# A four-layer transformer on one core: four weight products moved from the third feed-forward's shared tiles into the third attention, and one PSUM bank for both tiles of a pair there

## The reference

```
x = x + tanh(g_xattn[l]) * attention_l(layernorm(x), ctx)
x = x + tanh(g_ffn[l])   * ffn_l(layernorm(x))
```

```
scores = hidden[b] @ memory[b].T / 16 ; scores = where(mask, scores, -1e30)
attn = softmax(scores) ; out = attn @ memory[b]      (zero where no row is valid)
```

```
u = x @ Wup + bup
g = silu(u @ Wgate + bgate) * u
o = g @ Wdown + bdown
```

## Time and profile before

| | us |
|---|---|
| median of 3 runs | 967.28 (965.3 to 967.49) |
| profiled execution, its own time | 966.25 |
| its span, first to last instruction | 964.4 |
| TensorE matmul busy | 793.1 (82%) |
| VectorE busy | 619.4 (64%) |
| ScalarE busy | 427.7 (44%) |
| GpSimd busy | 330.3 (34%) |
| mean granted TensorE clock | 0.874 |

### The profile page before, as it was taken

The page is one execution under the profiler, slowest core; times in us unless marked ns, Lnnn a source line. Parts: engine busy times, 40 slices in busy tenths (PEclk is TensorE's granted clock), DMA queues, the critical chain, the costliest instruction groups (busy, mean ns, idle before and its releaser), DMA issues.

```text
span 964.4 us, 16889 instructions
## 1 busy us (share of the span) xinstructions
PE 793.1 (82%) x4572; PEld 512.1 (53%) x4572; DVE 619.4 (64%) x1467; ACT 427.7 (44%) x932; POOL 330.3 (34%) x598
## 2 busy tenths in 40 slices
PE   0599998988882268888879997999996989999990
PEld 0445554444441144658568875656664845666650
DVE  8488997678866757657522237378885777444445
ACT  0456666567760012223127765666664313333320
POOL 3000002235636542023855765200002484233340
PEclk9799999989996569555799997899999599999995
DMA  9410006999108960005444536200003122223217
GB/s 327 127 23 21 21 12 192 305 305 314 39 12 336 320 183 1 0 0 197 130 134 138 153 104 195 72 20 20 19 7 119 52 89 83 61 79 91 87 37 261
DMA packets 90278, 113.00 MB, mean 117 GB/s; under 512 B 11685, under 2 KB 81864, under 8 KB 89050
## 3 DMA queue, kind: packets, MB, share of 16 engines
q1 hardware_dynamic: 83434, 95.20, 32.6%
q0 software_dynamic: 6768, 16.86, 4.9%
HBM read 51.10 MB, written 58.42 MB: 114 GB/s over the span
## 4 chain that ended last, share of the span: by engine, by line
PE 60%; DVE 15%; issue 8%; ACT 7%; POOL 6%; DMA 2%; DVEq 1%; SPq 1%; POOLq 0%; ACTq 0%
PE ps L2084 9%; PE ps L1670 7%; PE ps L1660 6%; PE ps L2104 4%; PE ps L1975 4%; PE ps L1681 3%; POOL x_rows L547 3%; PE ps L1993 2%; PE ps L1968 2%; PE ps L1706 2%; PE ps L2051 2%; PE ps L1880 2%; PE ps L1893 2%; PE ps L1657 2%; PE ps L1693 1%
## 5 line engine op out<-in xcount | busy, mean ns | idle before, releaser
L769 ACT ACTIVATE probs_t<-ps 128x1024 f32<-128x1024 f32 x64 | 65.5, 1024 | 71.1 <-PE ps L1670 71.1
L611 POOL COPY work<-ctx_rows 128x256 f32 (+1 forms) x32 | 12.7, 399 | 212.1 <-PE ps L1681 212.1
L1149 DVE TENSOR_REDUCE row_max<-ps 128x8 f32<-128x1024 f32 x64 | 77.9, 1217 | 4.6 <-issue 2.4
L1155 DVE TENSOR_TENSOR work<-ps,row_max 128x1024 f32<-128x1024 f32 x64 | 77.7, 1214 | 3.4
L1512 DVE TENSOR_TENSOR ctx_cols<-ps,ctx_rows 128x512 f32<-128x512 f32 x54 | 37.3, 691 | 59.9 <-PE ps L2084 59.7
L1015 ACT ACTIVATE ctx_cols<-ctx_cols 128x256 f32<-128x256 f32 x54 | 22.5, 417 | 117.1 <-DVE ctx_cols L1512 117.1
L1670 PE MATMUL ps<-ident,work 128*128 128x128 f32 x512 | 70.0, 280 | 2.3 <-ACT work L763 2.1
L2084 PE MATMUL ps<-early,xt 128*128 x152 | 71.5, 593 | 0.0
L1670 PEld LDWEIGHTS ps<-ident,work 128*128 128x128 f32 x512 | 56.7, 142 | 17.3 <-ACT work L763 13.1
L588 POOL DMA_INDIRECT y_rows<-ctx_cols,w2d x38 | 37.5, 988 | 80.7 <-DMA y_rows<-ctx_cols,w2d 47.1
L2104 PE MATMUL ps<-early,ctx_cols 128*128 (+1 forms) x216 | 55.8, 381 | 4.2 <-ACT ctx_cols L1020 4.2
(11 more groups left out here) (331 smaller groups left out, 1977.5 us busy)
## 6 DMA issues: line engine op xcount, KB each, us to landing
x_rows<-pad_row SPq DMA_DIRECT2D x1, 17415.0 KB, 66.8
work<-x_rows SPq DMA_DIRECT2D x77, 129.0 KB, 2.1
x_rows<-pad_row SPq DMA_DIRECT2D x1, 7740.0 KB, 35.3
x_rows<-pad_row SPq DMA_DIRECT2D x1, 7611.0 KB, 92.2
early<-in_w3st SPq DMA_DIRECT2D x8, 512.0 KB, 6.2
work<-y_rows SPq DMA_DIRECT2D x16, 256.0 KB, 2.9
early<-y_rows SPq DMA_DIRECT2D x8, 512.0 KB, 7.3
late<-in_w2u SPq DMA_DIRECT2D x1, 2304.0 KB, 9.7
```

Source lines behind the costliest of these rows:

```text
L769: act.activation(probs_t[:, :, :], ps[:, 4:6, :], ACT.Copy).then_inc(sem("att.evac"), 1)
L1149: dve.tensor_reduce(row_max[:, u, 8 * c:8 * c + 8], scores(c), AX.X, ALU.max).then_inc(sem("att.max"), 1)
L1155: dve.tensor_tensor(probs[:, u, c, :].rearrange("p (h k) -> p h k", k=P), scores(c), row_max[:, u, 8 * c:8 * c + 8].unsqueeze(2).to_broadc ...
```

## The change

The first four products move out of the third feed-forward's loop. Each is cut into two halves (`fuse(e, halves)`); a half is one product with the bias rows and two with the weights. The first half of product 0 stands behind the first pair's scores; after that each pair's `attend_l2` holds one half, between the transposes and PV, except the last. ScalarE copies a product after the exponentials of the pairs t = 2, 6, 10 and 14. VectorE adds the four products' bias rows once, ahead of the router's `norm_rows`. The products use banks 2 and 3; both transposes of a pair now go to bank 5 and both PVs to bank 4, so ScalarE copies both transposes in one instruction, and VectorE's first add waits for both PVs. TensorE's and ScalarE's loops over the pairs are written out. The router's tiles 8 and 12, which use banks 2 and 3, wait for the last copy and the bias add.

```diff
         def fuse_bank(e):
-            return 6 if e < EARLY else e - EARLY
+            return 2 if e < EARLY else e - EARLY
+
+        def fuse_rows(e):
+            return ps[0:E3 + 1, 3 if e < EARLY else 7, 0:D]
...
             def evac_l2(t):
-                for u in range(2):
-                    act.wait_ge(sem("l2.tr"), t + u + 1)
-                    wait(act, sem("l2.pv"), t + u - 1)
-                    act.activation(pt_l2[:, u], bank(2 + u, P), ACT.Copy).then_inc(sem("l2.evac"), 1)
+                act.wait_ge(sem("l2.tr"), t + 2)
+                wait(act, sem("l2.pv"), t)
+                act.activation(pt_l2, bank(5, 2 * P).rearrange("p (s n) -> p s n", s=2), ACT.Copy).then_inc(sem("l2.evac"), 2)
...
-            tile_pairs(act, attention2, peel=2)
+                if t % 4 == 2:
+                    act.wait_ge(sem("kv.stored"), 32)
+                    product_out(t // 4)
+            for t in range(0, NT, 2):
+                attention2(t, t == 0, t == NT - 2)
...
-                if 5 <= i < 5 + EARLY:
-                    product_out(i - 5)
...
-                    dve.wait_ge(sem("l2.pv"), t + u + 1)
-                    add_gated(4, t + u, bank(4 + u, D), rc_l2[:, u:u + 1])
+                    dve.wait_ge(sem("l2.pv"), t + 2)
+                    add_gated(4, t + u, bank(4, (u + 1) * D, u * D), rc_l2[:, u:u + 1])
...
+            def add_rows(e):
+                upto(dve, "wp.mm", e + 1)
+                dve.tensor_tensor(brow[:, D:2 * D], fuse_rows(e), brow[:, D:2 * D], ALU.add).then_inc(sem("b3.row"), 1)
+
             dve.wait_ge(sem("kv.stored"), 32)
+            dve.wait_ge(sem("load.brow"), 32)
+            add_rows(EARLY - 1)
             for g in range(3):
                 norm_rows(5, xs2, g)
...
-                if i == 10:
-                    dve.wait_ge(sem("load.brow"), 32)
-                    add_rows(EARLY)
...
+            def fuse(e, halves=(0, 1)):
+                if 0 in halves:
+                    pe.wait_ge(sem(f"load.st{e % 4}"), 16 * (e // 4 + 1))
+                    if e == EARLY:
...
+                    elif 0 < e < EARLY:
+                        upto(pe, "wp.out", e)
+                up_t, ga = wst[:, e % 4, 0], wst[:, e % 4, 1]
+                for c in halves:
+                    mm(fuse_rows(e), bupz[:, e, c, :], ga[:, c, :], start=(e in (0, EARLY) and c == 0),
+                       stop=(e in (EARLY - 1, E3) and c == 1), skip_group_check=True)
+                    for j in range(2):
+                        op = mm(ps[:, fuse_bank(e), c * D:(c + 1) * D], up_t[:, j, c * P:(c + 1) * P], ga[:, j, :], start=(j == 0),
+                                stop=(j == 1))
+                if 1 in halves:
+                    op.then_inc(sem("wp.mm"), 1)
...
+            def attend_l2(t, half):
+                if t == 0:
+                    pe.wait_ge(sem("resid3"), NT)
+                wait(pe, sem("l2.evac"), t)
                 for u in range(2):
                     pe.wait_ge(sem("l2.exped"), t + u + 1)
-                    wait(pe, sem("l2.evac"), t + u - 1)
-                    pe.transpose(bank(2 + u, P), p_l2[:, u], ident[:, :]).then_inc(sem("l2.tr"), 1)
+                    pe.transpose(bank(5, (u + 1) * P, u * P), p_l2[:, u], ident[:, :]).then_inc(sem("l2.tr"), 1)
+                if half:
+                    fuse(half // 2, (half % 2,))
+                pe.wait_ge(sem("l2.evac"), t + 2)
+                wait(pe, sem("resid4"), t)
+                for u in range(2):
+                    mm(bank(4, (u + 1) * D, u * D), pt_l2[:, u], ctx_rows[:, t + u, :], start=True, stop=True).then_inc(sem("l2.pv"), 1)
...
+            for t in range(0, NT, 2):
                 for u in range(2):
                     front(4, t + u, u, lambda u: pe.wait_ge(sem("front.out"), FRONT[3] + NT))
-                if not first:
-                    attend_l2(t - 2, isinstance(t, int) and t == 2)
+                if t:
+                    attend_l2(t - 2, t // 2)
...
-            tile_pairs(pe, attention2, peel=2)
-            attend_l2(NT - 2)
+                if t == 0:
+                    fuse(0, (0,))
+            attend_l2(NT - 2, 0)
...
+                    if L == 5 and t == 7:
+                        upto(pe, "wp.out", EARLY)
+                    elif L == 5 and t == 11:
+                        pe.wait_ge(sem("b3.row"), 1)
...
-                if 4 <= i < 4 + EARLY:
-                    fuse(i - 4)
```

More of the change, by code:

```diff
@@ L888, in evac_l2, with product_out @@
             def evac_l2(t):
-                for u in range(2):
-                    act.wait_ge(sem("l2.tr"), t + u + 1)
-                    wait(act, sem("l2.pv"), t + u - 1)
-                    act.activation(pt_l2[:, u], bank(2 + u, P), ACT.Copy).then_inc(sem("l2.evac"), 1)
+                act.wait_ge(sem("l2.tr"), t + 2)
+                wait(act, sem("l2.pv"), t)
+                act.activation(pt_l2, bank(5, 2 * P).rearrange("p (s n) -> p s n", s=2), ACT.Copy).then_inc(sem("l2.evac"), 2)
+            def product_out(e):
+                upto(act, "wp.mm", e + 1)
+                act.activation(w13[:, e, :, D:2 * D], bank(fuse_bank(e)).rearrange("p (j n) -> p j n", j=2), ACT.Copy
+                               ).then_inc(sem("wp.out"), 1)
             def attention2(t, first, last):
@@ L918, in score @@
                                ).then_inc(sem("rt2.sig"), 1)
[L920 to L923, removed]
             route_in(5, score)
@@ L1465, in _ @@
             hidden2(2)
-            def add_rows(n):
-                upto(dve, "wp.mm", n)
-                dve.tensor_tensor(brow[:, D:2 * D], ps[0:E3 + 1, 7, 0:D], brow[:, D:2 * D], ALU.add).then_inc(sem("b3.row"), 1)
             for i in range(NT + 2):
@@ L1498, in _ @@
             dve.wait_ge(sem("b3.row"), 1)
-            add_rows(E3 + 1)
+            add_rows(E3)
             for t in range(2, NT, 2):
@@ L1868, in _ @@
             pe.wait_ge(sem("mask.add"), 1)
-            def attend_l2(t, first=False):
+            def fuse(e, halves=(0, 1)):
+                if 0 in halves:
+                    pe.wait_ge(sem(f"load.st{e % 4}"), 16 * (e // 4 + 1))
+                    if e == EARLY:
+                        upto(pe, "s2.x", N2)
+                        upto(pe, "m2.h", NT + N2)
+                        upto(pe, "m2.ht", NT + N2)
+                    elif 0 < e < EARLY:
[9 more added lines that the diff above has]
+                    op.then_inc(sem("wp.mm"), 1)
@@ L1871, in attend_l2 @@
+            pe.wait_ge(sem("load.brow"), 32)
+            def attend_l2(t, half):
+                if t == 0:
+                    pe.wait_ge(sem("resid3"), NT)
+                wait(pe, sem("l2.evac"), t)
                 for u in range(2):
                     pe.wait_ge(sem("l2.exped"), t + u + 1)
-                    wait(pe, sem("l2.evac"), t + u - 1)
-                    pe.transpose(bank(2 + u, P), p_l2[:, u], ident[:, :]).then_inc(sem("l2.tr"), 1)
-                for u in range(2):
[L1876 to L1880, removed]
@@ L1889, in attention2 @@
                     wait(pe, sem("l2.exped"), t + u - 1)
-                    pe.wait_ge(sem("mask.add"), 1)
                     mm(bank(u, P), ones3[0:1, :], mask_bf[0:1, t + u, :], start=True, stop=False)
@@ L1940, in router @@
                 pe.wait_ge(sem("front.out"), FRONT[L] + NT)
[L1942 to L1951, removed]
-                up_t, ga = wst[:, e % 4, 0], wst[:, e % 4, 1]
-                for j in range(2):
-                    mm(ps[0:E3 + 1, 7, 0:D], bupz[:, e, j, :], ga[:, j, :], start=(e in (0, EARLY) and j == 0),
-                       stop=(e in (EARLY - 1, E3) and j == 1), skip_group_check=True)
-                for c in range(2):
-                    for j in range(2):
-                        op = mm(ps[:, fuse_bank(e), c * D:(c + 1) * D], up_t[:, j, c * P:(c + 1) * P], ga[:, j, :], start=(j == 0),
-                                stop=(j == 1))
-                op.then_inc(sem("wp.mm"), 1)
             def turn_slot(L, s, xd):
```

1 line of the change is left out of this document (removed).

## The result

On the chip of the first measurement the changed kernel takes 978.27 us (median of 4 runs, 977.01 to 980.96), the kernel before 966.29 (4 runs, 965.07 to 967.49): ratio 1.0128, 95% interval [1.0099, 1.0156]. It was measured twice more, beside other experiments: 973.95 us (5 runs, ratio 1.0064 [1.0037, 1.0092]) and 975.54 us (6 runs, 1.0104 [1.0072, 1.0137]). The 15 runs have a median of 976.5 and reach from 970.0 to 981.7. It is slower, as forecast (974.5). Part of the spread has a cause that the profiles show (experiment 8).

A forecast was written before the change was run, and what follows sets the result against it. It took TensorE at the low clock to nearly fill the third attention's rounds, and the sends to pace the shared tiles. 966.25 + 3.3 (high-clock sum with restart) + 5.0 (low-clock rounds) = 974.6, stated as 974.5 us; range 964.5 to 983.

The forecast's parts named there:

- removal from the shared tiles: Third feed-forward's shared tiles: taking out 11.5 us of TensorE work gains 0, since the sends set the pace.
- half behind the transposes, a round: Third attention, high clock: the half product between second transpose and PV delays PV by 0.9 us a round.
- shared bank, a round, high clock: Third attention: VectorE's first add waits for both PVs, moving its later work by 0.46 us a round.
- clean round at the high clock: Third attention: a round carrying a half product takes 6.96 us at the high clock, against 5.62 before.
- three stalls for ScalarE's copy: Third attention: in three of six rounds TensorE waits for ScalarE's product copy, 0.35 us each, 1.05 together.
- parts at the low clock: Third attention: the clock is lost now and then, two of six rounds' worth at the low clock, +5.0 us.
- first PV, from the stage's first transposes: Third attention's start: product 0's two halves stand ahead of the first PV and delay it by 1.65 us.
- last PV to the first send: tail, bias add, router: Attention's end and router: -0.4 us tail, +0.41 bias add, -1 router's first tiles if the clock is still high.
- restart at the low clock: TensorE's restart behind the shared tiles: a longer pause may lengthen its low start, 0 to +1.8 us, taken as +0.4.
- rival 1: Third attention: the clock stays high all through, giving 969.6 us; chance 0.18.
- Rival 2: Third attention: the clock stays low all through, giving 986 us; chance 0.14 for low throughout or nearly.
- Rival 3: Third attention: half product falls into TensorE's wait, add-wait hidden, high-clock rounds 5.6 to 6.5 us, 958 to 963.5; chance 0.13.

The follow-up runs named there:

- experiment 8: The changed kernel, unaltered, measured and profiled a third time: 975.54 us, ratio 1.0104 to the kernel before.
- experiment 1: The kernel before without its first four products, their copies and the first bias add, nothing put elsewhere: 965.71 us, ratio 0.9989.
- experiment 3: The changed kernel with each half product ahead of the pair's transposes and ScalarE's product copy ahead of the exponentials: 967.7 us, ratio 1.0005.
- experiment 4: The changed kernel with the two PVs in separate banks again and both tiles' scores sharing bank 0: 969.13 us, ratio 1.0019.
- experiment 6: The changed kernel with the edits of experiment 3, experiment 4 and experiment 5 together: 963.83 us (ratio 0.9975), again 961.38 us (0.9938).
- experiment 2: The kernel before with only the bank edit (both transposes in bank 5, both PVs in bank 4), no product moved: 972.21 us, ratio 1.0053.
- experiment 5: The changed kernel with products 4 to 7 in the old bias-rows-first order and the bias add behind three norm_rows: 974.14 us, ratio 1.0074.

## Why the prediction was right, point by point

| step | predicted, us | measured, us |
|---|---|---|
| removal from the shared tiles | 0 | experiment 1: -2.1 to +0.1 (interval) |
| half behind the transposes, a round | +0.9 | +0.80 (experiment 3) |
| shared bank, a round, high clock | +0.46 | +0.43 to +0.44 (experiments 4, 6), +0.63 (experiment 2, one round) |
| clean round at the high clock | 6.96 | 6.87 |
| three stalls for ScalarE's copy | +0.35 each | +0.32 each |
| last round | 6.04 | 6.06, 6.04, 5.79 |
| parts at the low clock | +5.0 | +5.4, +5.4, +1.5 |
| first PV, from the stage's first transposes | +1.65 | +1.67 in all three |
| first PV, from the span's start | (same) | +1.9, +2.1, 0.0 |
| last PV to the first send: tail, bias add, router | -1.0 | -0.2 |
| restart at the low clock | +0.4 (0 to +1.8) | +1.0 |
| late products' order | none | +1.2 |

The stage was right in mechanism and nearly in size. From its first transposes to L1430 (L1434 in the changed kernel) it is 8.5 us longer in two profiles and 4.4 in the third, within the 4 to 12 that were to show. Where three numbers stand in a cell, they are the three profiles of the changed kernel, in order. The measured +5.4 is the 53.59 us from first to last PV, less the last round (6.06) and three clean rounds and three with a stall (3 x 6.87 + 3 x 7.19 = 42.18). "Two rounds' worth" came out as parts of four rounds. It was a choice between cases rather than a working, so that it fits the first two profiles is in part luck: the third (+1.5) shows that rival 1, the clock high throughout, nearly happened in one execution. Rival 2, low throughout, did not in any, and no round was low from end to end, so the price of such a round (9.5 us) was not measured. Against the kernel before on the same chip the medians are 12.0, 7.0 and 9.9 us slower; the forecast was 7.2.

The Trainium skill (TensorE: Matmul & The Clock Gate, Part 4: PE-mode transpose) says that transposes don't count as busy for the clock. The case that the prediction drew from it, low throughout, is in none of the three profiles; that speaks against the sentence here, but no run tests it by itself.

The sum for the second profile: 8.9 us at the first send (458.16 against 449.23), 8.7 at the restart, 9.7 after the routed tiles' low start, 10.9 behind the late products, and 10.7 at the end of the span; its own time, 977.01, is 10.8 over the 966.25 of before. The forecast had 8.3. Three terms were mis-sized. The router gained next to nothing, 0.2 us from the last PV to the first send where 1.0 stood: the clock was low from 442 us on, as it had been before, although the stage ahead of it was mostly at the high clock. The restart cost 1.0 us and not 0.4, and its reason was wrong: the low time doesn't follow the pause (last section). And the products were costed only in the place where they went; the same edit to `fuse` rewrote the four that stayed, by an order that stands in the diff, at 1.2 us.

Rival 3, which I gave 0.13, failed for the reason given against it: the half can't use TensorE's wait ahead of the transposes, because it stands behind them. Experiments 3, 4 and 6 show it from the other side. Each of the two edits alone brings the median back to within 0.2% of before, and the two together, with the products' old order, make the kernel 0.25 to 0.6% faster.

## What to carry to other kernels

Look for the idle time in the profile and put moved work ahead of the wait that makes it, not behind: here the same half product cost 0.80 us a round behind the transposes and nothing ahead of them, save once at the stage's start. Work taken out of a stage that another engine or a transfer paces is worth next to nothing, in both places tried here (11.5 us for at most 0.2%, and 11.5 us for 0.9). When the clock can be lost, read it before pricing a local saving: experiment 4's 3.3 us came with 8.6 against two profiles of the changed kernel and 4.5 against the third, by how long the clock was low in each.

## What the runs showed of the hardware

**The clock isn't told by busy time alone.** In the kernel before, rounds with TensorE busy 6.49 of 6.90 us stayed low for 44 us; in experiment 1 the same code was back at 1.00 for its last round. In experiment 4, four rounds with 20.43 us busy of 26.37 were at 1.00 throughout. In the changed kernel one execution held 1.00 over 26.71 us with 18.49 busy, and two others fell to 0.69 as the mean of a round. What decides which level a stretch gets was not settled by these runs.

**The low start after a pause does not grow with the pause.** The first 6 us of the routed tiles (windows of TensorE: busy, clock, DMA share, GB/s), of experiment 6 and of experiment 5:

```profile
496.45:502.45 6.00, 6.00 (x26) 0.77 0.42 114
```

```profile
508.61:514.61 6.00, 6.00 (x18) 0.51 0.42 113
```

Both stand behind 18.3 us of idle time, and one is low for 2.75 us, the other for 6. Before, with a pause of 4.3 us, it was 3.75; over ten profiles 2.75 to 6.0. Half of each such time is lost: the last routed tile came 66.9 us behind the restart after 2.75 us low, 67.3 after 3.75, 68.5 after 6.0. The Trainium skill (TensorE: Matmul & The Clock Gate, Part 1: The HAM clock gate) says that how many matmuls run cold at a kernel's start varies from run to run; these rows show the same of a restart inside a kernel.

**The order of narrow and wide products costs TensorE time.** The same twelve instructions took 2.89 us with the four on 8-column weights together and 3.18 us with them in two pairs between the 128-column ones: 0.29 us for two more switches in a product. A switch changes the width of the weights and also the PSUM bank that is written (7, or the product's own); which of the two costs was not tested.
